# First attention layer of a four-stage block run batch by batch, with the norms, gates and weight turning of batch 0 as pieces inside it

## What is computed

```
x = x + ln(attn0(ln(x)))     # 8 heads, score depth 64, value width 128, no mask
x = x + ln(moe(ln(x)))       # softmax gates, best 2 of 8 experts, and a shared expert
x = x + ln(attn1(ln(x)))     # 16 heads of 8, causal, with a slope per head
x = x + ln(ffn(ln(x)))       # two layers of local attention and a gated MLP
```

```
Q, K, V = x @ Wq.T, x @ Wk.T, x @ Wv.T        # V is 128 wide for each head
out = sum over heads of softmax(Q K.T) V      # the heads are added, not joined
scores = softmax(x @ gate_w.T)                # the gates; the two largest are kept
y = sum over e of (silu(w1 x') w2) * (w3 x') * mask_e,   z = silu(x sw1) * (x sw2) @ sw3
```

## Time and profile before

| | us |
|---|---|
| median of 3 runs | 1628.68 (1622.58 to 1630.45) |
| the profiled execution's own time | 1631.59 |
| its span | 1629.6 |
| opening, up to the first scores (L671) | 35.07 |
| 8 attention blocks and the last products, up to the turning of yT | 35.07 to 568.43 |
| norms, gates, shared expert, up to the first expert unit | 568.43 to 623.94 |
| all behind it | 623.94 to 1629.6 |

### The profile page before, as it was taken

The page is one execution under the profiler, slowest core; times in us unless marked ns, Lnnn a source line. Parts: engine busy times, 40 slices in busy tenths (PEclk is TensorE's granted clock), DMA queues, the critical chain, the costliest instruction groups (busy, mean ns, idle before and its releaser), DMA issues.

```text
span 1629.6 us, 25354 instructions
## 1 busy us (share of the span) xinstructions
PE 1382.9 (85%) x9075; PEld 827.6 (51%) x9075; DVE 1050.4 (64%) x2238; ACT 781.0 (48%) x1658; POOL 387.3 (24%) x268
## 2 busy tenths in 40 slices
PE   6999999999999949996799999872788767788766
PEld 4777777777777733332233333331455542455542
DVE  6767767667677564666666776408677645677644
ACT  2444445444444313341255666652677732677731
POOL 2000000000000011345300000002688801688801
PEclk9999999999999968998689999995899978899978
DMA  5000000000000000002023111002000000000000
GB/s 131 1 1 1 0 0 0 0 0 0 0 0 0 0 0 0 1 1 97 14 72 97 43 35 35 2 7 52 1 0 0 1 1 1 1 0 0 1 0 26
DMA packets 23650, 25.44 MB, mean 16 GB/s; under 512 B 5570, under 2 KB 20108, under 8 KB 22284
## 3 DMA queue, kind: packets, MB, share of 16 engines
q1 hardware_dynamic: 23580, 24.51, 5.2%
HBM read 20.11 MB, written 4.39 MB: 15 GB/s over the span
## 4 chain that ended last, share of the span: by engine, by line
PE 61%; POOL 16%; DVE 10%; issue 8%; ACT 3%; DMA 1%; POOLq 0%; SPq 0%; DVEq 0%; ACTq 0%
PE ps L640 14%; PE ps L671 8%; PE ps L682 7%; POOL d_rn L2145 5%; PE ps L952 4%; POOL probsT L2156 4%; PE ps L911 3%; PE ps L932 3%; POOL k_st L2143 2%; PE ps L788 2%; POOL q_st L2143 2%; PE ps L627 2%; PE ps L782 2%; PE ps L772 2%; PE ps L1152 1%
## 5 line engine op out<-in xcount | busy, mean ns | idle before, releaser
L1877 ACT ACTIVATE probsT<-ps 128x512 f32<-128x512 f32 (+1 forms) x304 | 163.5, 576 | 106.2 <-PE ps L936 93.2
L1268 DVE TENSOR_REDUCE negmax<-ps 128x1 f32<-128x1024 f32 x128 | 150.7, 1219 | 76.1 <-PE ps L671 76.1
L1722 ACT ACTIVATE probs<-ps,negmax 128x1024 f32<-128x1024 f32 x128 | 142.7, 1114 | 75.6 <-DVE negmax L1268 75.3
L1728 ACT COPY probsT<-ps 128x512 f32<-128x512 f32 x128 | 74.9, 585 | 177.9 <-PE ps L682 177.8
L682 PEld LDWEIGHTS ps<-ident,probs 128*128 128x128 f32 x1024 | 114.7, 141 | 58.4 <-issue 53.5
L911 PE MATMUL ps<-arena 76*128 76x512 bf16 (+3 forms) x384 | 113.6, 355 | 27.2 <-DVE cmax L1476 20.9
L682 PE MATMUL ps<-ident,probs 128*128 128x128 f32 x1024 | 136.3, 276 | 0.0
L640 PE MATMUL ps<-probsT,v_nat 128*128 128x256 f32 x554 | 129.9, 380 | 0.0
L671 PE MATMUL ps<-k_st,q_st 64*128 64x512 f32 x512 | 127.2, 615 | 2.2 <-DVE v_st L1247 1.4
L1946 ACT ACTIVATE probsT<-ps,d_nm,d_rn 128x128 f32<-128x128 f32 x256 | 113.2, 464 | 29.1 <-DVE d_nm L1608 29.0
L1476 DVE CUSTOM_DVE_ANT_0 k_st<-ps,rel 128x256 f32<-128x256 f32 (+7 forms) x128 | 96.8, 756 | 44.9 <-PE ps L911 43.4
(11 more groups left out here) (259 smaller groups left out, 2638.1 us busy)
## 6 DMA issues: line engine op xcount, KB each, us to landing
arena<-c_parts SPq DMA_DIRECT2D x32, 192.0 KB
arena<-c_parts SPq DMA_DIRECT2D x16, 128.0 KB
arena<-in_L_ffn_w_dram SPq DMA_DIRECT2D x3, 512.0 KB
c_parts<-probsT SPq DMA_DIRECT2D x2, 768.0 KB, 3.5
arena<-in_c_far_dram SPq DMA_DIRECT2D x16, 96.0 KB
c_parts<-work SPq DMA_DIRECT2D x2, 768.0 KB, 11.2
work<-in_L_ffn_wqkv_dram SPq DMA_DIRECT2D x1, 1536.0 KB
x_sb<-in_L_attn_x_dram SPq DMA_DIRECT2D x2, 512.0 KB, 4.8
```

Source lines behind the costliest of these rows:

```text
L1268: dve.tensor_reduce(negmax[:, u:u + 1], s2, AX_X, ALU.max, negate=True)\
L1722: act.activation(probs[:, u % NPB, :], s2, ACT.Exp, bias=negmax[:, u:u + 1], accum_out=rowsum[:, u:u + 1]).then_inc(s_a_exp, 1)
L1877: act.activation(c_p[:, kt % 2, j0:j0 + heads, q0 - kt * P:q0 - kt * P + n], ps[:, 4 + c % 2, 0:heads * n].rearrange("p (h n) -> p h n", n ...
```

## The change

- **Order of blocks.** The loop is gone, all 8 blocks are written out, and batch 0's four pairs come first, then batch 1's four. The weights are read from w0q, w0k and w0v in place; POOL's copies into wq_st, wk_st and wv_st are gone. So are the zero products before block 0 and the projections behind block 7.
- **Output.** Each quarter of a block's output lies in bank 6 alone (256 columns), and DVE copies or adds it after each quarter (L1376 for the first pair, an addition after that), four a block instead of two. Bank 7 is free for the pieces.
- **Pieces.** `a_piece(m, i)` stands at the end of step i of block m on PE, DVE and ACT. Numbered through as slots 8 m + i, 0 to 63: PE turns a group of expert weights in slots 2 to 10 and DVE copies it out of bank 7 in slots 3 to 11; batch 1's input norm stands in 14 to 21, batch 0's output norm in 36 to 40, its second input norm in 42 to 49, its gates in 50 to 63. Inverse roots inside are POOL's.
- **Opening.** Only batch 0 is loaded, measured, normed and turned before the first projection; batch 1's load is issued behind the attention weights. ACT copies w0q and w0k.
- **After attention.** PE turns one group of gate operands and goes to the shared expert of batch 0 at once. Batch 1's output norm, second input norm and gates stand between shared parts 0 to 3 and in units 0 to 14.
- **Weigh.** In steps 0, 1 and 2 of a block the products left from the block before are 5, 8 and 8; before they were 8, 7 and 6.

In the diff:

```
-            with pe.Fori(0, PAIRS) as p:
-                for b in range(BATCH):
...
-                        if i == 0:
-                            weigh(m - 1, 1 - b, 2, 1, 3, 8)
-                            weigh(m - 1, 1 - b, 3, 0, 0, 3)
...
+            for m in range(BLOCKS):
+                for i in range(QT):
+                    if i == 1:
+                        turn(m, 0)
+                    scores(m, i)
+                    if i == 0:
+                        weigh(m - 1, 2, 1, 3, 8)
+                    elif i == 1:
+                        turn(m, 1)
+                        weigh(m - 1, 3, 0, 0, 8)
...
+                    a_piece(m, i)
```

```
+            def turn_f(g):
+
+                if g == 0:
+                    pe.wait_ge(s_ld_f, 16 * 12)
+                    pe.wait_ge(s_w0t, 2)
                 else:
-                    pe.wait_ge(s_ft, g - 3)
+                    pe.wait_ge(s_ft, g)
...
+                        ins = pe.transpose(ps[:, 7, i * P:(i + 1) * P], fnat[:, 4 * g + i, :], ident[:, :])
+                ins.then_inc(s_fp, 1)
...
+                if 2 <= slot < 11:
+                    turn_f(slot - 2)
...
+                if 3 <= slot < 12:
+                    turned_f(slot - 3)
...
+                for g in range(HALF):
+                    if slot == 36 + 2 * g:
+                        out_stats(0, 0, g, 7)
+                        half_aggr(0, g)
+                    if slot == (37, 40)[g]:
+                        half_norm(0, 0, g, 7, spread_no("out", 0, 0, g))
...
+                if 60 <= slot < 63:
+                    gate_part(0, slot - 60)
```

```
             def shared(k):
...
                 if k == 0:
-                    act.wait_ge(s_G, 1)
+                    act.wait_ge(s_a_pv, 4 * BLOCKS)
```

More of the change, by code:

```diff
@@ new lines, in turn @@
+            def turn(m, u):
+                n = NU * m + u
+                pe.wait_ge(s_a_norm, n + 1)
+                for half, free in ((0, s_a_evA), (1, s_a_evB)):
+                    if n > 0:
+                        pe.wait_ge(free, n)
+                    for i in range(4):
+                        kt = 4 * half + i
+                        ins = pe.transpose(ps[:, 4 + half, i * P:(i + 1) * P],
+                                           probs[:, u % NPB, kt * P:(kt + 1) * P], ident[:, :])
+                    ins.then_inc(s_a_trans, 1)
@@ new lines, in gate, with turn_g @@
+            def gate(b, t0):
+                if t0 == 0:
+                    pe.wait_ge(s_xT, group_no(1, b, 1))
+                for t in range(t0, t0 + 4):
+                    ins = pe.matmul(ps[:, 7, t * E0:(t + 1) * E0], xT[:, (QT * b + t) * P:(QT * b + t + 1) * P],
+                                    gateT[:, :], start=True, stop=True)
+                if t0 == 4:
+                    ins.then_inc(s_logits, 1)
+            def turn_g(b, g, bank):
+                if g == 0:
+                    pe.wait_ge(s_G, b + 1)
+                for i in range(4):
+                    ins = pe.transpose(ps[0:STRIP, bank, i * P:(i + 1) * P], G[:, QT * b + 4 * g + i, :], ident[:, :])
+                ins.then_inc(s_gTp, 1)
@@ new lines, in _ @@
+            dve.memset(b4[:, :, :], 0.0).then_inc(s_ld_z, 1)
+            dve.memset(eps_c[:, :], EPS).then_inc(s_eps, 1)
+            in_stats(0, 0, 0)
+            in_stats(0, 0, 1)
+            ch.settle()
+            for t in range(QT):
+                ins = dve.bn_aggr(mv[:, t, :], stats[:, t, :])
+            ins.then_inc(s_var, 1)
+            dve.wait_ge(s_sd, 1)
+            ch.step(dve.reciprocal(rstd[:, 0:QT], sd[:, 0:QT]))
+            half_xn(0, 0, 0, 0)
+            half_xn(0, 0, 1, 0)
@@ L1425, in _ @@
+            units(0, UB, piece)
             shared(4)
@@ L1813, in _, with piece @@
                     shared_out(0)
+            mask(0)
             shared_out(1)
-            for g in range(NCH):
-                act.wait_ge(s_gTp, g + 1)
-                act.copy(gT[:, g * CH:(g + 1) * CH], ps[0:STRIP, 6 + g % 2, :]).then_inc(s_gT, 1)
-            mask(0)
-            units(0, UB, lambda k: None)
+            def piece(k):
+                if k == 4:
+                    half_in(1, 1, 0, 5)
+                    half_in(1, 1, 1, 6)
+                if k == 6:
+                    gate_exp(1)
+                if k == 14:
+                    turned_g(1, 0, 7)
+                    turned_g(1, 1, 5)
+            units(0, UB, piece)
             for k in range(4, 8):
```

918 lines of the change are left out of this document (517 added, 401 removed).

## The result

| | before | after |
|---|---|---|
| median of 10 runs | 1630.43 (1622.58 to 1633.67) | 1613.07 (1610.47 to 1619.61) |
| ratio after to before | | 0.9904, 95% interval 0.9887 to 0.9922 |
| profiled execution, span | 1631.59, 1629.6 | 1614.61, 1612.8 |
| first scores | 35.07 | 22.82 |
| last value product ends | 567.59 | 586.31 |

The change makes the kernel 1% faster, 17.4 us by the medians and 16.8 us of span. The forecast was 27.6, so 1601; the range, 1585 to 1621, holds the result. In differences from stage to stage: opening -12.25, attention +31.0 (563.5 us long, 532.5 before), from the last value product to the first unit -41.6 (14.8, 56.35 before), units of batch 0 with the parts behind them +6.3 (75.97, 69.71 before), all behind that -0.2. The forecast had -12.9, +23.8, -41.8 and +3.3 (the projections behind block 7, which it counted apart, are in the attention here).

A forecast was written before the change was run, and what follows sets the result against it. PE was taken as the bound in attention and units, waiting in the opening and between them. Terms -12.9 - 1.2 + 9.2 + 13.6 + 9.1 - 6.9 - 41.8 + 3.3 = -27.6 gave 1604.0 profiled, 1601 median; range 1585 to 1621.

The forecast's parts named there:

- rival B: Attention blocks and units: DVE's pieces delay PE, 0.5 us for each of 29, giving 1616; chance 0.20 shared with another rival.
- Opening: Start to first scores: one load fewer ahead of Wv, half of DVE's work, first scores near 22.2, -12.9 us.
- Block 0: First attention block: products on zeros go, but scores still wait for exponentials; -1.2 us (0 to -2.5).
- Bank 7: Slots 3 to 10: PE waits for DVE's copy of the previous expert weights from the single bank, +13.6 us.
- Rival A: Attention: the hand-over of the single bank costs nothing because DVE is early enough; 1587, chance 0.14.
- Starts of blocks: Before a block's first turning, 5 products leave PE waiting 1.3 us, in seven blocks: +9.1 us (5 to 11).
- Attention to units: Last value product to first expert unit: 56.3 us shrinks to 14.5, the DVE chain late next; -41.8 us.
- Units: Batch 0's expert units: added PE work and heavy DVE pieces, less some slow clock; +3.3 us (0 to +9).
- The clock's -2: First units: the slow clock cost about 4 us; with PE busy until shortly before, half is taken back.
- DVE's terms of 0.8 and 1: Units of batch 0: 0.8 us for norming 8 tiles and 1 us for the gates' pieces.
- ACT's two table loads: Switches between exponentials and silus in the units: 1.28 us each, covered by ACT's idle time but for 0.4.
- Rival C: Bank 6 for all quarters: each waits for the previous addition; at 1.1 us each 1635, slower than before; chance 0.06.

## Why the prediction was right, and where it was short

The stages and most terms came as forecast. The range held the result in part by its width: 1613 lies nearer to rival B's 1616 than to the forecast's 1601, and only the rows tell that B's mechanism is not what made the attention longer.

- **Opening**, forecast -12.9: measured -12.25. First scores were put at 22.2 and came at 22.82; Wv landed at 9.25, not 8.8.
- **Block 0**, forecast -1.2: by the profiles at the full level -1.3 (18.2 us to the fourth scores less 0.5 for a piece, against 19.0 before). But the products on zeros were what filled PE's waits of 3.5 and 2.7 us, and at the lower level the gain is lost again.
- **Bank 7**, forecast +13.6: measured 13.3 in eight waits with DVE's copy as releaser: 1.38 in slots 3, 5 and 7, 1.71 in 4 and 6, 1.11 and 1.44 in 9 and 10, against 1.5 and 1.85. The 3.21 of slot 8 stand where the forecast has two terms, 2.0 for the hand-over and 1.3 for the start of block 1. With the latter's share taken off, the hand-over is 12.2. Rival A is out.
- **Starts of blocks**, forecast +9.1: five waits of 1.15 and one of 0.71, where a piece fell into the gap, 6.5 us; with 1.15 of the wait in block 1, 7.6, within its bounds of 5 to 11. Both kinds of wait together were forecast 2.9 us too long (22.7 against 19.8).
- **Steady blocks**: blocks 2 to 6 came to 66.7 to 68.2 us, and the last with its tail to 70.6; the forecast had 67 to 70. The pieces from slot 36 on cost 3.3 us by the experiment without them, where PE's own work in them was put at 3.5. So PE's pieces are paid in full and DVE's cost nothing there. Rival B, DVE's pieces pushing PE, is out for the attention; in the units it struck, as below.
- **The term that was missing** is the clock in the attention. The forecast took the waits at their own length. It had the earlier trace rows before it, where the clock fell after idle stretches, and used that only for the units. Each wait of 1.7 us brought 1.6 us more behind it. Missed: 6.0 us in slots 4, 6 and 8, and 1.4 in block 0 of this profile, up to 4.3 in others. The attention was 7.2 us longer than forecast: 7.4 by the clock and 1.2 by bank 6, less the 2.9 of the waits; 1.5 us are left that no row was assigned to.
- **Attention to units**, forecast -41.8 with the first unit 14.5 us behind the last product: measured -41.6 and 14.8. The chain of DVE and POOL was late next, as said.
- **Units**, forecast +3.3: measured +6.3. The clock's -2 holds (from the first unit to the third L765 behind it 11.72 us before, to the third L851 9.95 after, so -1.8). With PE's own 3.5, which wasn't measured apart, 4.6 us are left for DVE and ACT. DVE's terms of 0.8 and 1 were short. The norming was priced by a row of 3.08 us, which itself held one such collision with POOL; here it met two and took 4.02, and PE lost 1.8 us in all there. The steps of the gates were taken at their length alone, without what POOL adds. Without POOL's additions the stretch is 3.4 us shorter. The Trainium skill ("SBUF — State Buffer", SBUF: two separate sides) states a mechanism for it: VectorE, in some of its forms that read SBUF, and GpSimd share a pair of ports as an exclusive lock, and the later one stands until the other is through. This case's trace agrees, with 1283 ns against 341 for one form and 203 as ever for another, the reciprocal; the prediction didn't weigh it.
- **ACT's two table loads**: rows of 1.28 us at 630.64 and 633.35, with the next activations 0.01 and 0.02 us behind them. PE waited 0.85 us for ACT at 635.48, and 1.0 us in all; the forecast by the row gave 0.4. The estimate from the Trainium skill ("ScalarE: Activation LUTs", What ACT_TABLE_LOAD costs), 2.66 us for a load and a drain, was 3 us more. The truth lies nearer to the row, and no drain is seen between load and activation.
- **Rival C**, bank 6 for all quarters: 30 of 31 quarters came in time. In a steady step DVE's addition ends at 267.45 and PE's products start at 269.17, a margin of 1.7 us where the forecast had 1.8. It struck once, for 1.2 us, where no scores stand between two quarters, behind block 7. The experiment with 8, 7, 6 shows how near it was: three products moved forward, and it costs 0.6 us in each of seven blocks.

## To carry to other kernels

A wait of an engine whose clock follows its activity can be dearer than its length: here 13.3 us of waits brought 6.0 more, and a wait of 1.71 us brought 1.6. Look whether the long rows behind it are the same work at the lower level. Where two engines hand a single bank to and fro, the taker's place in its queue decides; here the same transposes cost 19 us more in front of the next scores than behind them. Before a gain is put down to an edit, compare the rows that the edit doesn't touch: 2.7 of 3.4 us in the units were the level of the clock. When small steps are moved beside another stage's work, look up what each neighbour does at that moment, not only how busy the engine is.

## What was not expected of the hardware

- Behind idle times of 1.71 us, between stretches of work, TensorE fell from 2.4 to 1.2 GHz for some microseconds, twice in a profile: score products of 3.19 and 3.28 instead of 1.99 us. Behind those of 1.38 us it didn't. Dead products in their place kept the granted clock at 1.00.
- Some VectorE operations with both ends in SBUF, started while GpSimd adds, last until the addition is over: TENSOR_SCALAR 1283 against 341 ns, CAST 1261 against 195, TENSOR_TENSOR 1290 against 222. Without the additions the six casts take 194 to 195 ns. Statistics, MAX8, FIND_INDEX8 and RECIPROCAL on SBUF aren't stretched, and VectorE's steps that read PSUM in the same stretch kept their 0.69 and 0.75 us.
- The start of block 0 ran at either level, in kernels that are alike up to there, worth up to 4.3 us of a run (18.2 to 22.6 us to the fourth scores). What decides it isn't shown.
